# State-space stage: the decay matmul in two f16 parts for eight heads, the token norm applied at the accumulation, and groups of heads pipelined in a new order

## What is computed

```python
proj = hidden_states @ in_proj_w.T            # gate 4096, hbc 4096 + 2*1024, dt 64
conv = conv_bias + sum of 4 shifted taps of hbc; xBC = silu(conv)   # -> x, B, C
dt_p = softplus(dt + dt_bias);  A = -exp(A_log);  dA = exp(dt_p * A)
def step(state, inp):                          # scan over 64 tokens, 64 heads of 64 x 128
    state = state * dA_t[..., None, None] + dtx_t[..., None] * B_t[:, :, None, :]
    y_t = jnp.einsum('bhpn,bhn->bhp', state, C_t)
y = y + x * D
var = jnp.mean(yg * yg, axis=-1, keepdims=True)          # over the 512 channels of a group
yn = (yg * lax.rsqrt(var + EPS)) * norm_weight * silu(gate)
out = jnp.einsum('bli,di->bld', yn, out_proj_w)
```

## Time and profile before

| | us |
|---|---|
| median of three runs | 2626.93 (2626.21 to 2630.4) |
| profiled execution, its own time | 2626.67 |
| its span, first to last instruction | 2625.2 |
| TensorE busy | 2462.9 (94%) |
| VectorE busy | 2037.1 (78%) |
| ScalarE busy | 1266.3 (48%) |
| GpSimd busy | 1470.1 (56%) |

### The profile page before, as it was taken

One profiled execution on the slowest core, in us unless ns is written; L12 is line 12 of the kernel. 1 busy time (PEld: TensorE's weight loads), 2 busy tenths in 40 slices (PEclk: granted clock), 3 DMA queues, 4 the chain that ended last, 5 costly groups with the idle time before them and its releaser, 6 DMA issues. The chain is left out here.

```text
span 2625.2 us, 49059 instructions
## 1 busy us (share of the span) xinstructions
PE 2462.9 (94%) x18636; PEld 1767.0 (67%) x18636; DVE 2037.1 (78%) x2800; ACT 1266.3 (48%) x1837; POOL 1470.1 (56%) x895
## 2 busy tenths in 40 slices
PE   6879999999999999999999999999978889999994
PEld 3458787787787787787787787887853444444442
DVE  6867878887887888888788878877784478888884
ACT  4545545545544545545445445445443355544541
POOL 0116777777776777777777777767750022222321
PEclk9989999999999999999999999999998899999998
DMA  5520000000010010010010000000008311111100
GB/s 185 170 56 27 29 24 24 26 24 24 30 31 18 26 31 16 30 31 24 20 31 24 29 24 24 25 9 15 5 5 265 111 57 57 56 56 56 56 17 25
DMA packets 100293, 117.50 MB, mean 45 GB/s; under 512 B 7278, under 2 KB 69998, under 8 KB 100078
## 3 DMA queue, kind: packets, MB, share of 16 engines
q1 hardware_dynamic: 97806, 107.09, 12.6%
q0 software_dynamic: 2272, 7.50, 1.1%
HBM read 96.74 MB, written 17.83 MB: 44 GB/s over the span
## 5 line engine op out<-in xcount | busy, mean ns | idle before, releaser
L176 POOL TENSOR_TENSOR p_l<-S,p_h 128x1792 f16<-128x1792 f32 x126 | 422.4, 3353 | 289.8 <-ACT p_h L444 289.8
L550 DVE SCALAR_TENSOR_TENSOR S<-pS,rk,mask 128x256 f32<-128x256 f32 x832 | 359.8, 477 | 141.0 <-PE pS L244 134.3
L244 PE MATMUL pF<-w_h,ctx_h 128*128 128x256 f16 (+1 forms) x1664 | 454.5, 273 | 0.0
L244 PE MATMUL pF<-w_l,ctx_h 128*128 128x256 f16 (+1 forms) x1664 | 454.5, 273 | 0.0
L244 PE MATMUL pF<-w_h,ctx_l 128*128 128x256 f16 (+1 forms) x1664 | 454.3, 273 | 0.0
L560 DVE TENSOR_REDUCE mx<-S 128x256 f32<-128x3328 f32 x64 | 382.4, 5974 | 2.2
L244 PE MATMUL pF<-ctx_h,w_h 128*128 128x400 f16 (+1 forms) x1024 | 341.5, 333 | 4.0 <-PEq L789 4.0
L244 PE MATMUL pF<-ctx_l,w_h 128*128 128x400 f16 (+1 forms) x1024 | 341.5, 333 | 0.0
L244 PE MATMUL pF<-ctx_h,w_l 128*128 128x400 f16 (+1 forms) x1024 | 340.8, 333 | 0.0
L426 ACT ACTIVATE v_h<-pF 128x512 f16<-128x512 f32 (+1 forms) x224 | 126.8, 566 | 406.0 <-PE pF L244 406.0
L650 POOL TENSOR_TENSOR sq_l<-sq_f,sq_h 128x400 f16<-128x400 f32 (+1 forms) x256 | 242.9, 949 | 64.6 <-ACT sq_h L418 64.6
(11 more groups left out here) (242 smaller groups left out, 5599.2 us busy)
## 6 DMA issues: line engine op xcount, KB each, us to landing
ctx_p<-ctxT_dram SPq DMA_DIRECT2D x42, 458.0 KB, 3.5
s_wst<-winG_dram SPq DMA_DIRECT2D x8, 1536.0 KB, 10.5
q_wst<-wqT_dram SPq DMA_DIRECT2D x8, 1024.0 KB, 7.1
o_scratch<-o_st SPq DMA_DIRECT2D x32, 256.0 KB, 2.4
p_ost<-o_scratch SPq DMA_DIRECT2D x16, 512.0 KB, 6.4
p_wst<-woT_dram SPq DMA_DIRECT2D x16, 512.0 KB, 7.5
s_wst<-winG_dram SPq DMA_DIRECT2D x8, 1024.0 KB, 7.3
m_wost<-woutG_dram SPq DMA_DIRECT2D x8, 1024.0 KB, 5.5
```

The costliest lines, as they stand in the source:

```text
L176: eng.tensor_tensor(p_l[:, s % 2, t0:t1, :], S[:, s % 2, t0:t1, :], p_h[:, s % 2, t0:t1, :], ALU.subtract).then_inc(pl_ok, 1)
L244: mm = pe.matmul(out, x, y, start=first and j == 0, stop=final and j == 2)
L550: ins = dve.scalar_tensor_tensor(out=S[:, s % 2, t, :].rearrange("p (r q) -> p r q", r=REP), in0=bank[:, t % 2, :].rearrange("p (r q) -> p ...
```

## The change

- Decay: the exponents are scaled by 4 and split into two f16 parts (`ahl`). A ramp holds eight heads in 64 columns each (one batch, on the partitions of either half tile) for both parts, f16. `decay` is two f16 matmuls into one bank instead of two f32 ones for four heads each; the exponential divides by 4. `masked` multiplies each half of the mask in.
- Norm: the square sums are made on GpSimd from four chunks to one, and one f32 matmul with a single column of ones gives them by token on the partitions. VectorE turns them into mean squares, GpSimd raises them to -1/2, and `accumulate` multiplies by that factor as it adds into x1. y is thus split unnormalised. The norm weight goes into the output weights (`parN`), S_Y = 64 into dt and D. The square root, the reciprocal and `normalise` are gone.
- The low part of y moves from VectorE to GpSimd; y is kept by tile.
- All parameters are loaded once at the start by SyncE; VectorE copies a group's out.
- Order: `body` runs ten times, with steps of groups g, g - 1 and g - 2 in each. Tiles 2 and 3 of a group stand beside the next group's first chunks; two bodies a turn of the hardware loop.

```diff
         def loop(eng, body):
-            body(0)
-            with eng.Fori(1, G - 1) as g:
-                body(g)
-            body(G - 1)
+            body(0, 0)
+            body(1, 1)
+            with eng.Fori(2, G - 3, 2) as g:
+                body(g, 0)
+                body(g + 1, 1)
+            for g in range(G - 2, G + 2):
+                body(g, g % 2)
...
-                        pool.tensor_tensor(R[:, q, :, :], upto[:, :].unsqueeze(1).to_broadcast([P, 4, P]),
-                                           ag[:, t, 4 * q:4 * q + 4].unsqueeze(2).to_broadcast([P, 4, P]), ALU.mult).then_inc(r_ok, 1)
+            def ramp(g, t):
+                wait(pool, agc, 2 * g + 1)
+                wait(pool, d_ok, TT * g + t - 1)
+                pool.tensor_tensor(R[:, t % 2, :, :], upto_h[:, :].unsqueeze(1).to_broadcast([P, 2 * GH, TOK]),
...
+            def join_squares(g, t):
+                n = TT * g + t
+                wait(pool, sqy, n + 1)
+                pool.tensor_tensor(sqb[:, t % 2, 0:2, :], sqb[:, t % 2, 0:2, :], sqb[:, t % 2, 2:4, :], ALU.add).then_inc(sqa, 1)
+                wait(pool, sqa, n + 1)
+                pool.tensor_tensor(sqb[:, t % 2, 0, :], sqb[:, t % 2, 0, :], sqb[:, t % 2, 1, :], ALU.add).then_inc(sqs, 1)
...
+            def low(g, t):
+                wait(pool, yhi, TT * g + t + 1)
+                pool.tensor_tensor(yl[:, t, :, :], y[:, t % 2, :, :], yh[:, t, :, :], ALU.subtract).then_inc(ylo, 1)
...
+            def power(g):
+                wait(pool, msn, g + 1)
+                wait(pool, acc, TT * (g + 1))
+                pool.tensor_tensor(rs[:, :], rsm[:, :], half[:, :], ALU.pow).then_inc(rsy, 1)
...
-                pe.matmul(pD[:, :], after[:, :], R[:, q, :, :], start=True, stop=True).then_inc(d_ok, 1)
+                pe.matmul(pD[:, :], after_h[:, :], R[:, t % 2, 0:GH, :], start=True, stop=False)
+                pe.matmul(pD[:, :], after_h[:, :], R[:, t % 2, GH:, :], start=False, stop=True).then_inc(d_ok, 1)
...
-                for j in range(GCH):
-                    mm = pe.matmul(pS[:, t * P:(t + 1) * P], ones[:, :], sqb[:, t % 2, j, :], start=j == 0, stop=j == GCH - 1)
-                mm.then_inc(ssm, 1)
+                pe.matmul(pS[:, t:t + 1], sqb[:, t % 2, 0, :], ones[:, 0:1], start=True, stop=True).then_inc(ssm, 1)
...
+                for b in range(2):
+                    cols = slice(b * TOK, (b + 1) * TOK)
+                    i = dve.tensor_tensor(E[:, t % 2, :, cols], Ec[:, t % 2, :, :],
+                                          cbm[:, t % 2, cols].unsqueeze(1).to_broadcast([P, GH, TOK]), ALU.mult)
...
+                dve.tensor_tensor(y[:, t % 2, :, :], yt[:, t % 2, :, :], gate[:, par_g, :, t * P:(t + 1) * P], ALU.mult).then_inc(yg, 1)
...
-                dve.scalar_tensor_tensor(out=x1[:, t, :], in0=pO[:, :], scalar=1.0 / (S_Y * S_W), in1=x1[:, t, :],
+                dve.scalar_tensor_tensor(out=x1[:, t, :], in0=pO[:, :], scalar=rs[:, t:t + 1], in1=x1[:, t, :],
```

More of the change, by code:

```diff
@@ L689 @@
 S_O = 64.0
-S_Y = 16.0
+S_Y = 64.0
+S_A = 4.0
 GROUPS = 8
@@ L1302, in state_space @@
-        yh = sb("m_yh", [P, GCH, ND], F16)
-        yl = sb("m_yl", [P, GCH, ND], F16)
+        rsm = sb("m_rsm", [P, TT])
+        rs = sb("m_rs", [P, TT])
+        yh = sb("m_yh", [P, TT, GCH, P], F16)
+        yl = sb("m_yl", [P, TT, GCH, P], F16)
         bank = [ctx.enter_context(nc.psum_tensor(f"m_b{i}", [P, 512], F32)) for i in range(8)]
[L1305 to L1310, removed]
+        pI, pX, pD, pY, pO, pCB = (bank[0], bank[1], bank[3]), bank[2], bank[4], bank[5], bank[6], bank[7]
@@ L1311, in state_space @@
+        pS = pCB[:, 256:256 + TT]
+        (dtp, sp_dve, sp_act, dt_ok, wC_in, wC_hi, wC_lo, ip, gat, cv0, cvs, conv, silu, agc, xt, dx, cb, cm, r_ok, d_ok,
+         e_ok, m_ok, y_ok, yev, sqy, sqa, sqs, ssm, msn, rsy, yg, yhi, ylo, op, acc, nwc, dcp) = [sem(n) for n in (
+             "dtp sp_dve sp_act dt_ok wC_in wC_hi wC_lo ip gat cv0 cvs conv silu agc xt dx cb cm r_ok d_ok "
+             "e_ok m_ok y_ok yev sqy sqa sqs ssm msn rsy yg yhi ylo op acc nwc dcp").split()]
         par_in = sem("par_in")
-        taps = sem("taps")
+        par_ok = sem("par_ok")
@@ L1328, in _, with on @@
+        def on(f, g, lag, *rest):
+            if isinstance(g, int) and not 0 <= g - lag < G:
+                return
+            f(g - lag, *rest)
         @block.sync
         def _(sp):
[L1330 to L1334, removed]
-                wait(sp, wC_lo, g)
-                sp.dma_start(wost[:, :, :], w_out.rearrange("(k p) c -> p k c", p=P)).then_inc(wC_in, 16)
@@ L1463, in _ @@
             loop(pe, body)
-            squares(G - 1, TT - 2)
-            squares(G - 1, TT - 1)
-            for t in range(TT):
-                out_tile(G - 1, t)
         @block.scalar
@@ L1554, in _ @@
             loop(act, body)
-            close(G - 1)
-            for j in range(GCH):
-                high(G - 1, j)
         @block.vector
         def _(dve):
+            dve.tensor_copy(after_h[:, :], after[:, :])
+            for b in range(2):
+                half_p = slice(b * TOK, (b + 1) * TOK)
+                dve.tensor_copy(upto_h[half_p, :], upto[half_p, half_p])
+            dve.memset(half[:, :], -0.5)
             ln.vector(dve)
@@ new lines, in split_C @@
+            def split_C(g):
+                wait(dve, wC_hi, g + 1)
+                for j in range(GCH):
+                    i = dve.scalar_tensor_tensor(out=wol[:, j, :], in0=wost[:, j, :], scalar=parN[:, j:j + 1], in1=woh[:, j, :],
+                                                 op0=ALU.mult, op1=ALU.subtract)
+                i.then_inc(wC_lo, 1)
+                wait(dve, wC_lo, g + 1)
+                if isinstance(g, int):
+                    if g < G - 1:
+                        dve.tensor_copy(parN[:, :], prm[:, g + 1, bias_n + GCH:]).then_inc(nwc, 1)
+                else:
+                    dve.tensor_copy(parN[:, :], prm[:, bass.ds(g + 1, 1), bias_n + GCH:].rearrange("p o n -> p (o n)")).then_inc(nwc, 1)
@@ new lines, in taps @@
+            def taps(g, j):
+                n = CONV * g + j
+                wait(dve, cv0, n + 1)
+                acc_v = cv[:, j % 2, :].rearrange("p (b q) -> p b q", b=BATCH)
+                src = pI[(GCH + j) % 3][:, :].rearrange("p (b q) -> p b q", b=BATCH)
+                for m in range(1, TAPS):
+                    if m > 1:
+                        wait(dve, cvs, 2 * n + m - 1)
+                    tap = parT[:, j * TAPS + TAPS - 1 - m:j * TAPS + TAPS - m]
+                    i = dve.scalar_tensor_tensor(out=acc_v[:, :, m:], in0=src[:, :, 0:TOK - m], scalar=tap, in1=acc_v[:, :, m:],
+                                                 op0=ALU.mult, op1=ALU.add)
+                    i.then_inc(cvs if m < TAPS - 1 else conv, 1)
```

527 lines of the change are left out of this document (292 added, 235 removed).

## The result

The changed kernel takes 2546.02 us (median of 4 runs, 2543.32 to 2547.7), the kernel before 2626.93. Measured again beside the kernel before it took 2546.49 against 2626.39, a ratio of 0.9689 [0.9672, 0.9705]. The change saves 81 us, not the 107.5 of the forecast: the time fell inside the range, on the number of the second rival (2547) and not on the likeliest case (2519). The profiled execution took 2543.32 us.

What follows compares the result with a forecast made beforehand. TensorE was taken to bound the state-space stage: first group 44.8, seven periods of 47.5 and a tail of 29.5 make 406.8 us against 514.3, so 2626.67 - 107.5 = 2519 us, range 2502 to 2548 for 8 in 10.

Steps and rivals of the forecast that it cites:

- the second rival: Case 2, state-space stage: GpSimd and VectorE exclude each other, or stalls stay at 6.3; period 51.5, 2547 us, chance 0.23.
- the likeliest case: Case 1, state-space stage: TensorE bound with small stalls, 46.5 to 49.5 us a group; 2519 us (2512 to 2533), chance 0.60.
- TensorE's time: TensorE's work per state-space group without waits: 45.9 us, down from 53.7.
- the first group: From the stage's first input matmul until group 1's first chunk: 44.8 us, with 3.4 us wait for decay 0.
- what the order leaves as stall: TensorE's stalls per group in the new order: 1.6 us for 6.3, giving a period of 47.5 us.
- the fourth case: Slower than before: a ring from gating to decay 0 holds TensorE each group; period 65, 2641 us, chance 0.03.
- GpSimd's load: GpSimd's work per group with joins, low parts, ramps and power: some 17 to 22 us, covered as a load.
- VectorE: VectorE's work per group: about 40 us, down from 49.4, under TensorE's 45.9 by 6.
- the tail: Drain behind the seven periods: tiles 2 and 3, squares to power, four output tiles; 29.5 us, over 35 meaning wrong.
- Case 3: State-space stage: no stalls at all, 45.8 us a group; 2507 us, chance 0.13.
- Case 5: Decay matmuls: f16 decay costs f32's price, 5.2 us a group not saved; 2555 us, chance 0.01.

Runs made afterwards that it cites:

- run 3: Changed kernel with tile 0's ramp ahead of the low part on GpSimd, and squares of tiles 0 and 1 behind chunk 5 on TensorE: 2529.77 us, 0.9631.
- run 1: Changed kernel with the ramp of tile 0 ahead of the low part in GpSimd's list: 2536.23 us, 0.9654.
- run 2: Changed kernel with the closing group's squares of tiles 0 and 1 moved behind chunk 5 in TensorE's list: 2536.86 us, 0.9657.
- run 4: Changed kernel with VectorE's weight split A of 3072 elements cut into four instructions of 768: 2538.49 us, 0.9665.
- run 7: Changed kernel with the low part of y back on VectorE, a 128x512 subtraction per tile: 2532.13 us, 0.9641.
- run 11: Changed kernel with low part on VectorE, later squares, last group's output-weight split behind tile 3's gating, last four output tiles alternating between two banks: 2528.52 us, 0.9621.
- run 9: Kernel before with only the f16 decay over eight heads and its wide ramp, old order and norm: 2599.56 us, 0.9901.
- run 10: Changed kernel with all new steps but a group's four tiles behind its ten chunks, as in the old order: 2633.16 us, 1.0026.
- run 5: Changed kernel with ramp first, squares later, and weight split A in four VectorE instructions: 2540.02 us, 0.9668.

## Why the prediction was right and wrong

**Right: TensorE's time.** 45.9 us a group was forecast, 46.05 is what it needs when it is little disturbed (run 3). The two matmuls of a decay start 0.22 us apart; a sum of squares with one column holds TensorE 0.18 us where it does not wait (two sums, four records, in 0.36 us in run 3), so 0.7 us a group for the 1.0 forecast. In the changed kernel the row gives 46.9.

**Right: the first group.** The wait for the first ramp was put at 3.4 us; it is 3.39 (the row at 2090.73 above). The whole came out 1.3 long.

**Wrong: what the order leaves as stall.** This is the step that failed: 1.6 us a group, from decay 0 "0.5 us early or, if GpSimd is held once, 1.6 us late" and the first key-query product 0.3 to 1 us late. Idle time is 3.1 us a group. With the busy time 1.0 above the forecast, the 1.5 us more of idle time make the 2.5 us of 49.96 - 47.5. About half of the 3.1, 1.5 us a group, is the wait for joined squares, for which the layout had no wait at all. The ramp was late in three groups of seven, by up to 2.7 us, 0.9 a group on average; the key-query product was waited for 0.2 us in all. Runs 1, 2 and 3 show these two waits to be the loss: with both moved run 3 lands on the period that was forecast, 47.83 for 47.5.

For the ramp the cause is the exclusion that the text itself saw in the earlier trace rows and held to be a case of 0.23. The measurement that the forecast took from those rows, 0.3 us on one masking, was of a short partner, and the fourth case's worst low part was 3.2 us. What it left out is that the partner sets the price: beside a 3.35 us split a 1.15 us low part takes 2.76 to 4.26, by how early in the split it begins. Runs 1, 3, 4 and 7 each keep this meeting from delaying decay 0, in different ways, and each gives 8 to 17 us, by the stage 6.3 to 14.1. For the squares the cause is shown less far: joins and low parts stand in one queue on GpSimd, each stretched by VectorE's work beside it (join 1.17 for 0.72, low part 1.60 for 1.15), and cutting the long split took only 2.4 of the 10.8 us away. How much of it is the exclusion with shorter partners and how much the mere length of the queue was not separated.

The Trainium skill, page "SBUF — State Buffer", section "Who interferes with whom", says that the one that issues first holds the shared port pair for its whole instruction and that the order of issue decides who is blocked. The traces agree: split first (the changed kernel), the low part took 4.26 for 1.15; ramp first (run 1), the split took 4.3 for 3.35.

**GpSimd's load** was put at 17 to 22 us a group, by how much it is held up; it is 137.97 / 6 = 23.0, just over.

**Wrong in its size: VectorE.** 40 us a group was forecast, 44.9 measured. Per group, from the rows' totals over 2124 to 2474: gating 4 x 1.12 = 4.5 us for 2.8 to 3.3, and the output-weight split 34.3 / 7 = 4.9 us, for which 2.3 by elements and under 0.9 for its four pieces and the small copies had been put down. Both are two-input instructions that meet GpSimd's. "VectorE has 6 us to spare" was the argument for the likeliest case; it had about 2.

**Wrong: the tail.** 29.5 forecast, 36.0 measured, over the 35 that the text had named as its limit. The four output tiles are right, 3.69 apart for 3.6, and 16.15 in all with the first at 1.2 GHz for 14.5. The rest is ahead of them: the output-weight split stands at 2484.52 ahead of the skip of tile 3 and, beside GpSimd's work, takes 4.49 us, which the sum for the drain did not hold. That it alone makes the drain late is not shown: run 11, where it stands elsewhere, has 0.4 us from that.

**The rivals.** Case 2 gave the time, and its mechanism, ramps and other work late by the exclusion, was at work, shown for the ramp and argued for the squares; but it was priced as a period of 51.5 and an unchanged tail, while the truth is 49.96, a tail 6.5 longer and a first group 1.3 longer. So that 2547 met the time was luck: two errors cancelled. Case 3 is refuted: even run 3 has 1.8 us of idle time a group. Case 5 is refuted by the 0.22 us between decay matmuls. Case 4 did not come: the longest wait of TensorE in a period was 2.7 us.

**Where the gain comes from.** Decay alone 27 us (run 9). Without the new order the full set of steps gives no gain, and a small loss (run 10). So in the lists that were tried the steps come to 81 us only together with the new order. How much the order would give without the other steps was not tried, for the norm at the accumulation is what allows output tiles to run before a group's sum is known.

## What to carry to other kernels

Before moving a step from VectorE to GpSimd, list the longest two-input VectorE instruction that can stand beside it: what is left of that one when the step begins, not the step's own length, is the delay to plan for, and what is queued behind it on GpSimd pays as well. The queue that TensorE waits for should go ahead of the others, even if that makes VectorE the one who is blocked. Cutting the long instruction helped where GpSimd was the one waited for (8 us, run 4) and cost 10 us where it was not (run 5). Time a change of steps in the order that it will have: here the same steps gave nothing in the one serial list tried and 81 us in the pipelined one.

## What the runs showed of the hardware

- The exclusion changes sides with the order of start: a low part begun behind the split takes up to 4.26 us for 1.15 and ends 1.0 us behind it; a split begun behind a ramp takes 4.3 for 3.35.
- Cutting a VectorE instruction into four lets a waiting GpSimd instruction in at a seam: 3.35 us became 6.2 (run 4), and 7.8 on average with the ramp first (run 5).
- GpSimd takes 1.90 us for 1024 f16 elements, 0.72 for 256 f32 elements from two inputs, and 1.02 for a power on four elements, 2.44 for one on 13.
- An f32 matmul with one column, two records, holds TensorE 0.18 us.
- With waits of 4.0 to 6.33 us for squares in every group, and others of 2.4 to 3.2, the mean granted clock over six groups was 0.86, and matmuls behind the long wait stood 0.43 us apart for 0.22 (run 10); in the changed kernel, with no wait over 2.74 us in a period, it was 0.99.
